# A four-layer graph network on one core: eight runs of edges per partition, the join in its own group, a bias added on leaving PSUM, and batch statistics in one pass

## What is computed

```python
# a: attention with one head, then batch norm over the nodes
e = leaky_relu(a_src[src] + a_dst[dst]);  alpha = softmax of e over the edges of each dst
out = segment_sum(alpha * h[src], dst) + bias
mean = jnp.mean(out, axis=0); var = jnp.mean((out - mean) ** 2, axis=0)
y = relu((out - mean) * rsqrt(var + eps) * gamma + beta)
# b: attention with four heads and a term from edge_attr_13, then + bias + x, layer norm, relu
# c: agg = segment_sum(edge_attr_128, dst); a three-layer perceptron on [x, agg, u]
# d: relu(x @ W_self.T + b + segment_sum((x @ W_rel[edge_type])[src], dst) / degree)
```

## Time and profile before

| | |
|---|---|
| median of 3 runs | 7520.71 us (7515.51 to 7521.68) |
| the profiled execution | 7515.34 us, span 7513.5 us |
| POOL busy | 5175.2 us, 69% of the span |
| DVE, ACT, PE busy | 3315.7, 995.6, 773.2 us |
| indirect DMAs of the three edge stages | 3 x 1568 |

### The profile page before, as it was taken

The page is one execution under the profiler, slowest core; times in us unless marked ns, Lnnn a source line. Parts: engine busy times, 40 slices in busy tenths (PEclk is TensorE's granted clock), DMA queues, the critical chain, the costliest instruction groups (busy, mean ns, idle before and its releaser), DMA issues.

```text
span 7513.5 us, 22080 instructions
## 1 busy us (share of the span) xinstructions
PE 773.2 (10%) x2744; PEld 515.6 (7%) x2744; DVE 3315.7 (44%) x5046; ACT 995.6 (13%) x3171; POOL 5175.2 (69%) x5364
## 2 busy tenths in 40 slices
PE   1100000000003670000000000128601000000000
PEld 1100000000002540000000000114300000000000
DVE  8355656556566634333343333486322222222223
ACT  2122222222221220000000000055200000000000
POOL 5777777777774457777777777551277777777776
PEclk7555555555555555555555555559855555555555
DMA  5367676676764323334333333234533333333332
GB/s 182 93 217 220 210 223 215 218 220 210 223 215 144 96 83 100 114 112 119 112 116 115 112 119 113 90 100 159 191 103 108 103 105 107 103 109 103 106 106 87
DMA packets 287594, 1048.37 MB, mean 140 GB/s; under 512 B 101818, under 2 KB 118206, under 8 KB 236494
## 3 DMA queue, kind: packets, MB, share of 16 engines
q1 hardware_dynamic: 108452, 670.60, 24.9%
q0 software_dynamic: 175968, 373.53, 19.5%
q10 hardware_dynamic: 3024, 2.83, 0.1%
HBM read 530.44 MB, written 516.12 MB: 139 GB/s over the span
## 4 chain that ended last, share of the span: by engine, by line
POOL 42%; issue 14%; PE 6%; DVE 5%; DMA 1%; POOLq 0%; ACT 0%; DVEq 0%; SPq 0%; ACTq 0%
POOL edge_rows L1049 20%; POOL edge_rows L1916 20%; POOL node_sums L1217 2%; PE ps L1821 2%; PE ps L327 1%; PE ps L330 1%; DVE stats L1526 1%; PE ps L1808 1%; POOLq L167 0%; PE ps L1859 0%; PE ps L868 0%; PE ps L1481 0%; DMA node_sums<-sums_a,sum_row 0%; DVE node_sums L1299 0%; PE ps L300 0%
## 5 line engine op out<-in xcount | busy, mean ns | idle before, releaser
L1916 POOL DMA_INDIRECT edge_rows<-table_rel,rel_row x1568 | 1479.5, 944 | 612.0 <-issue 477.6
L1049 POOL DMA_INDIRECT edge_rows<-table_b,src_i x1568 | 1503.7, 959 | 477.9 <-issue 477.9
L1049 POOL DMA_INDIRECT edge_rows<-table_a,src_i x1568 | 1484.4, 947 | 477.9 <-issue 477.9
L1137 DVE TENSOR_TENSOR z<-edge_rows,dst_logit 128x16 f32<-128x16 f32 (+1 forms) x196 | 41.3, 211 | 1959.2 <-DMA edge_rows<-table_b,src_i 1149.9
L1982 DVE TENSOR_TENSOR edge_rows<-edge_rows,ps 128x2048 f32<-128x2048 f32 x97 | 221.9, 2287 | 1470.4 <-DMA edge_rows<-table_rel,rel_row 1470.4
L1109 ACT ACTIVATE edge_rows<-edge_rows,weight_decay 128x129 f32<-128x129 f32 x1552 | 465.2, 389 | 0.0
L1142 DVE TENSOR_TENSOR ps<-edge_rows,ps 128x2064 f32<-128x2064 f32 (+1 forms) x194 | 451.8, 2329 | 0.2 <-issue 0.2
L1176 DVE TENSOR_TENSOR edge_rows<-edge_rows,ps 128x2064 f32<-128x2064 f32 (+1 forms) x194 | 450.4, 2322 | 0.0
L772 PE MATMUL ps<-ident,edge_rows 128*128 128x128 f32 x32 | 7.2, 420 | 3535.3 <-DVE edge_rows L1185 2041.4
L1100 ACT ACTIVATE ps<-weight_decay 128x128 f32<-128x128 f32 x97 | 27.3, 281 | 1900.6 <-DVE weight_decay L1180 1900.6
L1947 ACT ACTIVATE ps<-keep 128x16 f32<-128x16 f32 x97 | 19.5, 202 | 1904.8 <-DVE edge_rows L1982 1901.0
(11 more groups left out here) (265 smaller groups left out, 3582.9 us busy)
## 6 DMA issues: line engine op xcount, KB each, us to landing
sums_a<-edge_rows SPq DMA_DIRECT2D x99, 2064.0 KB, 7.9
sums_b<-edge_rows SPq DMA_DIRECT2D x99, 1120.0 KB, 4.5
edge_rows<-in_ea SPq DMA_DIRECT2D x98, 1024.0 KB, 11.8
sums_rel<-edge_rows SPq DMA_DIRECT2D x98, 1024.0 KB, 4.1
table_rel<-rel SPq DMA_DIRECT2D x98, 512.0 KB, 2.7
edge_rows<-table_a,src_i POOLq DMA_INDIRECT x1568, 4.0
edge_rows<-table_b,src_i POOLq DMA_INDIRECT x1568, 2.6
edge_rows<-table_rel,rel_row POOLq DMA_INDIRECT x1568, 2.5
```

What stands on the lines that cost most here:

```text
L1049: e.indirect_dma_start(out=rows[:, s, k, 0:L.W], out_offset=None, in_=L.table, in_offset=bass.IndirectOffsetOnAxis(ap=src[:, at:at + 1], a ...
L1916: e.indirect_dma_start(out=rows[:, s, k, :], out_offset=None, in_=table_rel, in_offset=bass.IndirectOffsetOnAxis(ap=rel_row[:, at:at + 1], ...
```

## The change

Four edits.

1. `GK = 8` strands per partition of 196 edges each. A group is still 16 gathers: `GS = 2` consecutive edges ("columns") of 8 strands. `NV` becomes 1024, so every tile of the crossing halves, and `p_head` issues 8 indirect DMAs. The running sum along a strand now takes two dependent half-wide steps a group.
2. The join is done in the group's own iteration: logits and maxima of both columns, the exponentials, then column 0 is joined to column 1 of the group before and column 1 to column 0. In the crossing the PSUM banks are laid out so that the second turn and the second `decays` wait for no copy, `v_add` of the plain crossing comes ahead of the last two DVE operations, and the copies read PSUM in the order of the row.
3. The table's bias is no longer a matmul: DVE copies PSUM out (`v_rows`), adding a bias tile whose head columns also hold the 1. ACT's `s_copy` and DVE's `v_fill` go from this table.
4. Batch statistics in one pass: the first chunk's mean is taken off all chunks with the bias (`first_mean`), squares are made and summed chunk by chunk in the first loop, and the variance is the mean square less the squared mean; the pass over all chunks between the loops goes, and the mean is folded into `beta`.

```diff
+GK = 8
+GS = GC // GK
-    NV = P * GC
+    NC = NG * GS
+    NV = P * GK
@@ t_project
-                e.wait_ge(*self.copied.at(k))
+                e.wait_ge(*(self.copied if self.bias is None else self.filled).at(k))
...
-                if self.bias is not None:
-                    i = e.matmul(at, ones[0:1, :], self.bias[:, :], start=False, stop=True)
@@ Table
+        def v_rows(self, e, k):
+            L, WX = self.L, self.WX
+            e.wait_ge(*self.projected.at(k + 1))
+            if k >= 2:
+                e.wait_ge(*self.stored[k % 2].at(16 * (k // 2)))
...
+            for i, n, at in parts:
+                done = e.tensor_copy(self.node_l[:, k * JB + i:k * JB + i + n, :], at[:, :, L.W:WX])
+            done.then_inc(self.copied.sem, 1)
+            for i, n, at in parts:
+                done = e.tensor_tensor(self.rows[:, k % 2, i:i + n, :], at[:, :, 0:L.W],
+                                       bc(self.bias[:, :].unsqueeze(1), [P, n, L.W]), ALU.add)
+            done.then_inc(self.filled.sem, 1)
@@ attention_edges, gpsimd
-                    e.wait_ge(*summed.at(g - NS + 1))
+                    e.wait_ge(*summed.at(g - NS + 2))
@@ attention_edges, vector (new loop)
+                for t in range(GS):
+                    join(g, t)
@@ nodes_a_stage, vector
+            def first_mean():
...
+                e.wait_ge(*first_summed.at(1))
+                t = then(e.tensor_scalar(mean[:, :], ps[:, 4, 0:D], 1.0 / count, None, ALU.mult))
+                e.wait_ge(*step.at(t))
+                then(e.tensor_tensor(bn_par[:, 0, :], bn_par[:, 0, :], mean[:, :], ALU.subtract))
+                e.tensor_tensor(chunk(agg, 0), chunk(agg, 0), over_nodes(mean[:, :]), ALU.subtract).then_inc(biased.sem, 1)
...
-            for k in range(NK):
-                e.tensor_tensor(chunk(agg, k), chunk(agg, k), over_nodes(mean[:, :]), ALU.subtract
-                                ).then_inc(centred.sem, 1)
@@ nodes_a_stage, tensor
+                    e.wait_ge(*squared.at(k))
+                    column_sums(k - 1, square[:, (k - 1) % 2, :, :], 1).then_inc(squares_summed.sem, 1)
```

More of the change, by code:

```diff
@@ L769, in t_turn @@
         def t_turn(self, e):
-            for k in range(GC):
+            for k in range(GK):
                 bank, at = bank_of(k)
@@ L1012, in attention_edges @@
+        free = {"state": states_free, "state2": states_free, "decay": decay_free, "xs": xs_free, "head": head_free}
+        heads_of_strands = head[:, 0:GK * L.WS].rearrange("p (k w) -> p k w", k=GK)
+        tail = rows[:, last, GC - GK:GC, :]
         beside = None
-        if attr is None:
-            state, free["state"] = slots[3]
-        else:
-            state, free["state"] = state2[:, NV + 1:2 * NV + 2], state2_free
+        if attr is not None:
             attrs = rows[:, :, :, L.W:L.WS]
-            half = GC // 2
@@ L1026, in attention_edges @@
-        crossing = SoftmaxCrossing(
-            L, sb, spread if L.AE else spread_a, rows[:, last, :, :], state, state2, decay,
-            xs[:, 0:GC * L.WN].rearrange("p (k w) -> p k w", k=GC), head.rearrange("p (k w) -> p k w", k=GC), free, beside)
+            beside = Crossing("beside", tail[:, :, L.W:L.WS], xs[:, GK * L.WN:GK * L.WN + NV + 1], decay[:, NV:2 * NV],
+                              heads_of_strands[:, :, L.W:L.WS], (6, 0), xs_free, decay_free)
+        crossing = SoftmaxCrossing(L, sb, spread if L.AE else spread_a, tail, states[:, 0:NV + 1],
+                                   states[:, NV + 1:2 * NV + 2], decay,
+                                   xs[:, 0:GK * L.WN].rearrange("p (k w) -> p k w", k=GK), heads_of_strands, free, beside)
@@ new lines, in attr_plus, with join @@
+            def attr_plus(g, t):
+                if g == 0 and t == 0:
+                    return
+                now = steps(rows[:, g % NS, :, :])[:, t, :, L.W:L.WS]
+                e.wait_ge(*step.at(attr_step[-1]))
+                done = e.tensor_tensor(now, now, old_attr, ALU.add)
+                if t == GS - 1:
+                    done.then_inc(attr_summed.sem, 1)
+                else:
+                    attr_step.append(then(done))
+            def join(g, t):
+                if g == 0 and t == 0:
+                    return
+                now = steps(rows[:, g % NS, :, :])[:, t, :, 0:NW]
+                if t == 0:
+                    e.wait_ge(*summed.at(g))
+                elif join_step:
+                    e.wait_ge(*step.at(join_step[-1]))
+                if H == 1 and g == 0:
+                    e.wait_ge(*weighted.at(1))
+                decay_now = factors[:, 1, t * GK:(t + 1) * GK, :]
+                done = then(e.tensor_tensor(heads(old), heads(before(g, t)), bc(decay_now.unsqueeze(3), [P, GK, H, C + 1]),
+                                            ALU.mult))
+                if H == 1:
+                    e.wait_ge(*weighted.at(g + 1))
+                e.wait_ge(*step.at(done))
+                done = e.tensor_tensor(now, now, old, ALU.add)
+                if t == GS - 1:
+                    done.then_inc(summed.sem, 1)
+                else:
+                    join_step.append(then(done))
@@ L1459, in residual @@
                                        ).then_inc(x_ready.sem, 1)
-            for i in range(NK + 5):
-                if inside(i - 5):
-                    table.v_fill(e, i - 5)
+            for i in range(NK + 4):
+                if inside(i - 4):
+                    table.v_rows(e, i - 4)
                 if inside(i - 3):
```

548 lines of the change are left out of this document (289 added, 259 removed).

## The result

The changed kernel takes **7333.39 us** (median of 4 runs, 7328.93 to 7335.80) where before takes 7521.10 (7515.51 to 7521.68) beside it: ratio 0.9751, 95% interval 0.9734 to 0.9768. On another chip it was 7345.97 against 7530.53, ratio 0.9754 (0.9738 to 0.9770). The profiled span falls from 7513.5 to 7327.1 us, by 186.4; the prediction's sum was 179.8.

The account below looks back on a forecast made before the run. POOL's indirect DMAs were taken to bound the edge stages, PE the table loop of nodes a. Savings summing to 179.8 us took 7515.3 to 7335.5, or 7341 against the median; forecast's own range 7318 to 7362, wider range 7308 to 7388.

Parts of the forecast that it names:

- end of edges a, landing to crossing: From the last gather's landing to the crossing in edges a: 21.3 us become 13.3, saving 8.0.
- crossing a; store: Crossing of edges a: 69.1 us become 32.5, saving 36.6; its last store, at half the bytes, saves 2.0.
- end of edges b; crossing b; store: Edges b: landing to crossing 13.0 to 9.6 us, crossing 63.7 to 28.8, store 1.0 less.
- end of edges rel: End of the rel stage: eight head gathers of 16 go, 10.1 us, half the store 1.0; saved 11.0 in all.
- first loop of nodes a: First loop of nodes a, with squares and first chunk's mean added: 1 us longer, bounds -5 and +12.
- statistics, to the first residual: Between the loops of nodes a: 29.5 us from last column sums to first squares operation become 6.8, saving 22.7.
- table loop: Nodes a, first scatter to end of last: 183.0 us become 128, saving 55.0, with POOL the longest at 8.9 a chunk.
- Steady state: nothing: Loops of the edge stages: no gain, DVE's 13 to 15 us a group hidden behind 20.2 us of fetching.
- the rival at 3%: Edges a: DVE becomes the bound once a group exceeds 20.2 us; slower than before from 22.0; chance 3%.
- Crossings halve: Crossings of edges a and b: links halve with NV, saving 36.6 and 34.9 us.
- the first rival: Table loop stays long, 43 us more, 7384 in all, as three engines lie within 0.7 us; chance 14%.
- The residual operations block POOL: Table loop: DVE's residual operations hold POOL 3 x 1.09 us a chunk, 43 us more, 7384 in all; chance 14%.

Follow-up runs that it names:

- more_dve_a: The changed kernel with each product of attributes in edges a computed five times on DVE; 8211.49 us (one run).
- joined_b: The kernel before, with a group's join done in the same group, in edges b alone; 7528.68 us (one run).
- runs_of_4: The changed kernel with four runs of edges per partition instead of eight (GK 4, GS 4); 7314.95 us, ratio to before 0.9715.
- two_pass: The changed kernel with the two-pass statistics of the kernel before, without the first chunk's mean; 8108.64 us, ratio to before 0.9816.
- runs_of_4_no_shift: The changed kernel with four runs per partition and squares taken without the first chunk's mean; 8254.23 us, 1.0004 of before.

## Why the prediction was right

Each step, predicted and measured (the rows are those above and the prediction's), in microseconds saved in the profiled execution:

| step | predicted | measured |
|---|---|---|
| end of edges a, landing to crossing | 8.0 | 7.7 |
| crossing a; store | 36.6; 2.0 | 36.7; 2.4 |
| end of edges b; crossing b; store | 3.4; 34.9; 1.0 | 3.5; 36.2; 1.4 |
| end of edges rel | 11.0 | 11.8 |
| first loop of nodes a | -1.0 | -3.4 |
| statistics, to the first residual | 22.7 | 24.6 |
| first residual to first scatter | 6.2 | 6.4 |
| table loop | 55.0 | 56.1 |
| sum | 179.8 | 183.4 |

The rest of the 186.4 is 1.4 in the stage ahead of edges a, which I left out, 1.2 in the loop of edges b, 0.9 in the last stage, and 0.2 or less elsewhere. I have no cause for these.

- *Steady state: nothing.* Right: POOL's gathers keep their 0.95 us and a group its 20 us, and the rival at 3% needed 6.6 us more of DVE a group than there was. The price that I gave it (98 us for each us above) was not tested: `more_dve_a` ran on a chip where POOL waits for DVE in edges a without any addition.
- *Crossings halve.* Right in sum, with errors that cancel in a. The copies take 1.23 us and not 1.8; the chain's waits between engines are longer than the 0.3 I gave them. For b, 28.8 was not what I said it was: 32.5 less a turn, a copy and a return of 1.8 each is 27.1. It took 27.5, and with luck, since its second spread found the clock at 1.00 and took 1.88 us, where a's took 3.57 at 0.50. In rel the sum hides two errors: the gathers gave 12.5 us and not 10.1, because one of the 16 before lasted 4.25 us beside DVE's scan and the longest of the eight 1.78, and the halved store gave nothing (5.0 us from its issue to the next stage, 4.7 before) where I had 1.0. `joined_b` and `runs_of_4` separate the two edits as the prediction did: join, tail; runs, crossing.
- *Statistics.* The missing 1.9 us are the column sums: I gave them the 3.4 us of the lower clock, and they took 1.6 at the granted clock of 1.00, behind a fuller first loop of PE (its clock's mean was 0.83 from 2450 to 2480; before, 0.57 from 2450 to 2500); that the one brought the other is argued. My four small operations stand behind the first one on the squares, not ahead of it; to the residual that changes nothing. `two_pass` shows the term undone. The first loop's loss of 3.4 is over my +1, within its bounds; 1.8 to 3.2 of such a loss go with `first_mean` in `runs_of_4_no_shift`. I had said 2 of its 5 us would be slack.
- *Table loop.* The end is right (126.9 us, 128 predicted) because POOL is the bound and its period was read from a row. What lies under it was mis-sized: I gave seven projections half the time of seven pairs, 5.4 us, and PE 8.2 a chunk; they take 3.7 and less, because the one-row matmuls had slowed the 128-row ones beside them and held the clock down. And `v_rows` was 0.3 + 1.3 where I had 0.4 + 1.5. So the three engines are not within 0.7 us of each other as I argued for the first rival, but at 8.9 (POOL) and 7.8 (DVE), with PE well behind.
- *The residual operations block POOL* (14%) did not come in its price, but its mechanism is there, and I had read it off a mean. Ten scatters start while such an operation (both inputs in SBUF) is under way, and each of them ends 0.84 or 0.85 us after that operation does. Over the table loops of ten runs, before among them, 90 scatters do so within 0.84 to 0.88 us; the 15 that do not started within 0.05 us of the operation.

```profile
2542.52 1.08 DVE L1532 TENSOR_TENSOR agg<-agg,bn_scale 128x896 f32<-128x896 f32 x1
...
2543.33 1.12 POOL L1463 DMA_INDIRECT dst_logit_b<-node_logit_b,start_row  x1 [0.30 <-issue]
```

  Nine of the ten take 1.11 to 1.23 us and one 1.89, the others 0.96 to 0.99. A scatter that was already under way when the operation began is not lengthened. So POOL loses 2.4 us in the whole loop, and not the 43 of the rival, because at most one scatter of a chunk meets an operation in that way, mostly near its end. On this the Trainium skill (SBUF — State Buffer, "SBUF: two separate sides") speaks of an exclusive lock in which whoever starts second is blocked: these rows, like the earlier trace rows, agree, and the prediction's words that the row of the loop shows something else were wrong.

## What to carry to other kernels

A serial piece between stages whose links go by elements is worth cutting by the number of elements, and pays for longer work in a stage that another engine bounds; but count the steps that this buys, for on a chip where operations start 0.7 or 1.4 us apart in long stretches the same edit, carried one step on, gave all of it back. Of the versions run, four runs per partition is fastest on one kind of chip (7314.95) and, without the first chunk's mean, no better than before on the other. Don't alternate one-row matmuls with full ones: put them together, ahead, one per bank.

## What I had not expected of the hardware

- An indirect DMA on POOL that starts while DVE works on two inputs in SBUF ends 0.84 to 0.88 us after DVE's operation does, 90 times out of 90 once 0.05 us of the operation have passed; one that started first is not lengthened.
- A one-row matmul in turn with 128-row ones: 0.77 us from one to the next at a granted clock of 0.50, against 0.48 for 128-row ones at the same level, and the clock never rose in 183 us.
- Two kinds of chips: before 7521 and 7531 us on two, 8260 and 8248 on two others. The group of gathers in edges a, in the changed form, on either kind:

```profile
L1073 POOL DMA_INDIRECT edge_rows<-table_a,src_i x1568 | 1483.4, 946 | 477.9 <-issue 477.9
```

```profile
L1073 POOL DMA_INDIRECT edge_rows<-table_a,src_i x1568 | 1487.4, 949 | 710.5 <-issue 475.5 <-DVE edge_rows L1191 235.0
```

  The second is from `two_pass`: a gather itself takes no longer, but POOL waits 235 us for its slots. In edges b and rel a gather's own mean is 1.06 and 1.02 us there and 0.96 and 0.94 on the first. Why operations of DVE and ACT start 0.70 or 1.40 us apart there, dependent or not, and only in some stretches, is open.
- A DVE copy that reads PSUM in strides and writes in one run: 1.23 us for 1024 elements (1.2 ns each); the other way round 3.58 for 2048 (1.75 ns each).
